# Score groups in pairs, one FFN sum bank and one projection per pair of steps in a macaron block on one core

## What is computed

```
x = x + 0.5 * ffn(layernorm(x), w_gate_up, w_proj)       # FFN "A"
x = x + attention(layernorm(x), Wq, Wk, Wv, Wo)          # sliding window of 128, blocks of 128 tokens
x = x + 0.5 * ffn(layernorm(x), w_gate_up, w_proj)       # FFN "C", the same weights

ffn:       gate, up = split(x @ w_q(gate_up).T);  h = silu(gate) * up
           out = rms_norm(h) @ w_q(proj).T
attention: scores of a block of 128 queries against the keys of its own and the block before
           (the first block of each 512 tokens only against its own), mask, softmax, times v, @ Wo.T
```

## Time and profile before

| | |
|---|---|
| median of 3 runs | 2030.6 us (2028.21 to 2031.13) |
| profiled execution | 2030.56 us, span 2028.7 us |
| PE busy | 1919.7 us, 95% |
| PE weight loads | 898.9 us, 44% |
| DVE busy | 1541.2 us, 76% |
| ACT busy | 1493.1 us, 74% |
| POOL busy | 510.9 us, 25% |
| mean granted TensorE clock | 0.980 of 2.4 GHz |

### The profile page before, as it was taken

One profiled execution on the slowest core, in us unless ns is written; L12 is line 12 of the kernel. 1 busy time (PEld: TensorE's weight loads), 2 busy tenths in 40 slices (PEclk: granted clock), 3 DMA queues, 4 the chain that ended last, 5 costly groups with the idle time before them and its releaser, 6 DMA issues. The chain is left out here.

```text
span 2028.7 us, 37471 instructions
## 1 busy us (share of the span) xinstructions
PE 1919.7 (95%) x12447; PEld 898.9 (44%) x12688; DVE 1541.2 (76%) x4079; ACT 1493.1 (74%) x2871; POOL 510.9 (25%) x559
## 2 busy tenths in 40 slices
PE   6678899999999999999999999999999999999887
PEld 3353344444444444444444444444444444444332
DVE  8966788777876888777777888777786788777673
ACT  6837777777776777777776777777776777768672
POOL 2012222232223222322222223222223232221100
PEclk8889999999999999999999999999999999999898
DMA  7336888788887878777896788878886788768772
GB/s 233 121 71 112 147 153 147 132 141 159 149 156 126 156 145 153 136 145 150 154 159 125 138 155 153 149 131 154 159 155 120 141 153 165 144 120 154 131 136 52
DMA packets 1031648, 287.81 MB, mean 142 GB/s; under 512 B 1016096, under 2 KB 1017120, under 8 KB 1030944
## 3 DMA queue, kind: packets, MB, share of 16 engines
q1 hardware_dynamic: 1031456, 285.41, 75.9%
HBM read 25.17 MB, written 8.39 MB: 17 GB/s over the span
## 5 line engine op out<-in xcount | busy, mean ns | idle before, releaser
L731 ACT ACTIVATE masked<-masked,exp_bias,exp_scale 128x256 f32<-128x256 f32 (+1 forms) x1024 | 503.8, 562 | 8.6
L1095 PE MATMUL ps_yy<-wp_t,ht 128*128 128x512 bf16 x1978 | 481.0, 383 | 14.4 <-DMA ht<-hh 11.7
L1049 PE MATMUL ps_gu<-wgu_t,xt_A 128*128 128x512 bf16 x1940 | 473.8, 382 | 11.2 <-DVE hid L859 2.5
L1049 PE MATMUL ps_gu<-wgu_t,xt_C 128*128 128x512 bf16 x1958 | 472.6, 379 | 5.3 <-DMA xt_C<-xh 0.5
L605 ACT ACTIVATE hh<-hid 128x512 f16<-128x512 f32 x256 | 161.0, 629 | 276.3 <-DVE hid L865 271.0
L876 DVE CUSTOM_DVE_ANT_0 masked<-ps_s,mask 128x256 f32<-128x256 f32 (+1 forms) x1024 | 337.4, 385 | 0.7 <-PE ps_s L1085 0.6
L865 DVE SCALAR_TENSOR_TENSOR hid<-ps_gu,h_scale_u,hid 128x512 f32<-128x512 f32 x252 | 188.9, 750 | 185.0 <-PE ps_gu L1049 184.7
L1095 PEld LDWEIGHTS ps_yy<-wp_t,ht 128*128 128x128 f16 x2016 | 197.9, 99 | 254.5 <-DMA ht<-hh 13.5
L1049 PEld LDWEIGHTS ps_gu<-wgu_t,xt_A 128*128 128x128 f16 x2048 | 198.6, 98 | 243.3 <-issue 6.3
L1049 PEld LDWEIGHTS ps_gu<-wgu_t,xt_C 128*128 128x128 f16 x2048 | 193.4, 98 | 222.5 <-issue 2.4
L850 DVE TENSOR_TENSOR prob<-masked,prob 128x1024 f16<-128x1024 f32 (+1 forms) x256 | 278.9, 1089 | 2.4 <-ACT prob L743 2.4
(11 more groups left out here) (148 smaller groups left out, 1892.8 us busy)
## 6 DMA issues: line engine op xcount, KB each, us to landing
stream<-in_L_attn_x_dram SPq DMA_DIRECT2D x32, 256.0 KB, 3.3
pt<-prob SPq DMA_TRANSPOSE x512, 3.2
out_dram<-stream SPq DMA_DIRECT2D x32, 256.0 KB, 2.4
prob<-in_L_ffn_w_gate_up_dram SPq DMA_DIRECT2D x4, 1024.0 KB, 5.6
ht<-hh SPq DMA_TRANSPOSE x256, 3.3
stream<-in_L_ffn_w_gate_up_dram SPq DMA_DIRECT2D x3, 1024.0 KB, 5.6
stream<-in_L_ffn_w_proj_dram SPq DMA_DIRECT2D x2, 1024.0 KB, 4.9
prob<-in_L_ffn_w_proj_dram SPq DMA_DIRECT2D x2, 1024.0 KB, 4.8
```

Of the source, the lines that this page charges most:

```text
L731: t = act.activation(p, p, ACT.Exp, bias=exp_bias[:, 4 * g + h:4 * g + h + 1], scale=exp_scale[:, 0:1])
L1049: t = pe.matmul(bank[:, :], xt[s][:, part, k, :], wgu_t[:, k, at:at + CH], start=(k == 0 and part == 0), stop=(k == KD - 1 and part == 1))
L1095: t = pe.matmul(ps_y[s][:, :], ht[:, n % HRING, i, :], wp_t[:, 4 * c + i % 4, :], start=(c == 0 and i == 0), stop=(c == NC - 1 and i == 2 ...
```

## The change

It issues the scores of two groups, g even and g + 1, together at the end of every odd step, the first into the two banks of ps_s, the second into ps_x and ps_m. ps_x is the bank that C's sum had; both FFNs now sum in ps_y, and the first down of a block waits for the addition of the block before. ps_m is also the projections' bank: the projections move to even steps (Q 8, K 10, V 12, output 22), wait for the maxima of both groups, and scores wait until the projection of the step before has been taken. Values stand in mid-step, between down and up. DVE's order in a step becomes: low half of the projection or its addition, maxima of the even group, low half of the output, gate's product, low half of the probabilities, maxima of the odd group, normalising, FFN addition, product with up, LayerNorm statistics, low half of hidden. Normalising stands in the step of the values. The output's split, transpose and projection stand in one step (22), and SP issues its transpose ahead of the probabilities'. Cut to its core:

```diff
-    Q_AT, K_AT, V_AT = 8, 9, 11
+    Q_AT, K_AT, V_AT = 8, 10, 12
     SCORES = 12
     PROB = SCORES + 1
     PV = SCORES + 2
-    NORM = PV + 1
-    SPLIT_O, WO_AT = NORM + 7, 23
-    LN_C, XHAT_C, SPLIT_C = 24, 25, 26
+    NORM = PV
+    SPLIT_O, WO_AT = NORM + 8, 22
+    LN_C, XHAT_C, SPLIT_C = 23, 24, 26
-    LAST_WO = 8 * LAST + WO_AT
+    LAST_WO = 8 * LAST + WO_AT + 1
...
-        ps_y = {"A": ps_yy[:, 0:CH], "C": ps_yy[:, CH:2 * CH]}
+        ps_y, ps_x = ps_yy[:, 0:CH], ps_yy[:, CH:2 * CH]
         ps_om = psum("ps_om", [P, 2 * CH])
         ps_o, ps_m = ps_om[:, 0:CH], ps_om[:, CH:2 * CH]
+        ps_sc = ((ps_s[:, 0:CH], ps_s[:, CH:2 * CH]), (ps_x, ps_m))
...
+                b = block_at(step, SPLIT_O)
+                if b is not None:
+                    sp.wait_ge(d_ol, b + 1)
+                    need(sp, p_wo, b)
+                    transpose(ot[:, :, :, :].rearrange("p a b c -> p (a b) c"), flat(oh[:, :, :]), t_o)
                 b, g = group_at(step, PROB)
...
-                if block_at(step, SPLIT_O) == LAST:
-                    output_hi(LAST)
+                b = block_at(step, SPLIT_O)
+                if b is not None:
+                    output_hi(b)
                 s, b, c, n = gate_at(step)
                 if s:
                     tanh_half(s, b, c, n)
...
+                b = block_at(step, WO_AT + 1)
+                if b is not None and b < LAST:
+                    add_output(b)
+
+                b, g = group_at(step, SCORES)
+                if b is not None and g % 2 == 0:
+                    masked_max(b, g)
+                b = block_at(step, SPLIT_O)
+                if b is not None:
+                    take_lo(oh[:, 1, :], o_norm[:, :], oh[:, 0, :], a_oh, b + 1, d_ol)
...
+                s, bf, c, n = gate_at(step)
+                if s:
+                    gated(s, bf, c, n)
+
+                b, g = group_at(step, PROB)
+                if b is not None:
+                    need(dve, t_pl[g % 2], 16 * (4 * b + g // 2))
+                    take_lo(prob_part(prob[:, g % 2, 1, :, :, :], b), prob_f32(b, g),
+                            prob_part(prob[:, g % 2, 0, :, :, :], b), a_ph, 8 * b + g + 1, d_pl)
+                b, g = group_at(step, SCORES)
+                if b is not None and g % 2 == 0:
+                    masked_max(b, g + 1)
+                b, g = group_at(step, NORM)
+                if b is not None and g % 2:
+                    normalise_o(b, g // 2)
...
+                b = complete("A", step, 2)
+                if b is not None:
+                    add_ffn("A", b, d_x1)
+                b = complete("C", step, 2)
+                if b is not None:
+                    add_ffn("C", b, d_x3)
...
-            def output_projection(b):
+            def output_projection(b, step):
                 pe.wait_ge(t_o, 16 * (b + 1))
                 need(pe, d_v, min(b + 2, NB))
                 need(pe, d_x2, b)
-                project(O, ot, p_wo)
+                need(pe, d_mx, 2 * groups_by(step + 1, SCORES))
+                project(O, ot, p_wo, ps_m)
+
+            def projections_taken(step):
+
+                for offset, done in ((Q_AT, d_q), (K_AT, d_k), (V_AT, d_v), (WO_AT, d_x2)):
+                    b = block_at(step, offset)
+                    if b is not None:
+                        pe.wait_ge(done, b + 1)
...
-                        need(pe, d_x1 if s == "A" else d_x3, b)
+                        _, s0, b0, _ = QUARTERS[place(step - 2) - 1]
+                        pe.wait_ge(d_x1 if s0 == "A" else d_x3, b0 + 1)
                     down(s, b, c, place(step - 2))
...
-                s, b, c = ffn_at(step)
-                if s:
-                    if sb_:
-                        pe.wait_ge(d_h[sb_], 4 * bb + cb + 1 + (NC if sb_ == "A" else 0))
-                    up(s, c, 1, ps_u)
-
-
-                b, g = group_at(step + 1, SCORES)
-                if b is not None:
-                    if step + 1 == SCORES:
-                        pe.wait_ge(a_lo, 8)
-                    need(pe, d_mx, 2 * groups_by(step, SCORES))
-                    if g == 0:
-                        pe.wait_ge(t_q, 16 * (b + 1))
-                        pe.wait_ge(t_k, 16 * (b + 1))
-                    scores(b, g)
 
                 b, g = group_at(step, PV)
...
+                s, b, c = ffn_at(step)
+                if s:
+                    if sb_:
+                        pe.wait_ge(d_h[sb_], 4 * bb + cb + 1 + (NC if sb_ == "A" else 0))
+                    up(s, c, 1, ps_u)
+
+
+                b, g = group_at(step + 1, SCORES)
+                if b is not None and g % 2 == 0:
+                    if step + 1 == SCORES:
+                        pe.wait_ge(a_lo, 8)
+                    need(pe, d_mx, 2 * groups_by(step, SCORES))
+                    projections_taken(step - 1)
+                    if g == 0:
+                        pe.wait_ge(t_q, 16 * (b + 1))
+                        pe.wait_ge(t_k, 16 * (b + 1))
+                    scores(b, g, ps_sc[0])
+                    scores(b, g + 1, ps_sc[1])
...
                 b = block_at(step, K_AT)
                 if b is not None:
                     pe.wait_ge(a_q, b + 1)
                     pe.wait_ge(d_q, b + 1)
-                    project(K, xt["B"], p_k)
+                    need(pe, d_mx, 2 * groups_by(step + 1, SCORES))
+                    project(K, xt["B"], p_k, ps_m)
...
```

More of the change, by code:

```diff
@@ L298, in macaron @@
         assert len(AT_STEP) == len(GATES) == 2 * NB * NC - NC
+        assert all(QUARTERS[n][1:3] == QUARTERS[n - n % NC][1:3] for n in range(len(QUARTERS)))
         def gate_at(step):
@@ L946, in step_of, with add_output @@
             def step_of(step):
[L947 to L953, removed]
+                def add_output(b):
+                    dve.wait_ge(p_wo, b + 1)
+                    dve.scalar_tensor_tensor(out=slot(b), in0=ps_m[:, :], scalar=out_scale[:, 0:1], in1=slot(b),
+                                             op0=ALU.mult, op1=ALU.add).then_inc(d_x2, 1)
                 b = block_at(step, Q_AT + 1)
@@ L993, in step_of @@
                         attention_weight(n)
-                b = block_at(step, WO_AT + 1)
-                if b is not None and b < LAST:
-                    add_output(b)
+                b = complete("A", step, 2)
[4 more added lines that the diff above has]
+                    add_ffn("C", b, d_x3)
                 s, bf, c = ffn_at(step)
@@ L1012, in step_of @@
                                       ALU.subtract, ALU.mult).then_inc(d_xh, 1)
-                b = block_at(step, SPLIT_O)
-                if b is not None and b < LAST:
-                    output_lo(b)
-                b = complete("A", step, 2)
-                if b is not None:
-                    add_ffn("A", b, d_x1)
-                b = complete("C", step, 2)
-                if b is not None:
-                    add_ffn("C", b, d_x3)
                 b = block_at(step, LN_B)
@@ L1069, in attention_weight, with project, scores @@
                 t.then_inc(a_tr, 1)
-            def project(m, tokens, done):
+            def project(m, tokens, done, bank):
                 for k in range(KD):
                     for n, (part, w) in enumerate(((0, wat_hi), (0, wat_lo), (1, wat_hi))):
-                        t = pe.matmul(ps_m[:, :], tokens[:, part, k, :], w[m][:, k, :], start=(k == 0 and n == 0),
+                        t = pe.matmul(bank[:, :], tokens[:, part, k, :], w[m][:, k, :], start=(k == 0 and n == 0),
                                       stop=(k == KD - 1 and n == 2))
                 t.then_inc(done, 1)
-            def scores(b, g):
+            def scores(b, g, banks):
                 at_block = b % BPS
@@ L1250, in step_of @@
                     pe.wait_ge(a_k, b + 1)
+                    pe.wait_ge(d_q, b + 1)
                     pe.wait_ge(d_k, b + 1)
+                    need(pe, d_mx, 2 * groups_by(step + 1, SCORES))
                     if b == 0:
                         pe.wait_ge(a_lo, 8)
-                    project(V, xt["B"], p_v)
+                    project(V, xt["B"], p_v, ps_m)
                 b = block_at(step, WO_AT)
                 if b is not None and b < LAST:
-                    output_projection(b)
+                    output_projection(b, step)
             for step in range(FIRST_STEP, STEPS):
```

37 lines of the change are left out of this document (10 added, 27 removed).

## The result

The changed kernel takes 2213.4 us in the median of four runs (2212.3 to 2215.3), the kernel before 2030.8: a ratio of 1.0912, 95% interval 1.0898 to 1.0926. It is slower, as forecast, but by 183 us and not by 116; 2213 lies above the range of 2065 to 2200. The profiled execution took 2213.36 us with a span of 2211.3 us and a mean granted clock of 0.973.

The account below looks back on a forecast made before the run. The matrix engine's own list of work was taken as the bound. Waits of 131 us in 28 blocks plus 12 at the ends, less 27 saved at score bursts, added 116 to 2030.56: 2147 us, range 2065 to 2200.

Parts of the forecast that it names:

- Q: Projection in step 0 of 8: LayerNorm statistics lengthen the vector engine's chain to 12.71, a wait of 0.89 us.
- K: Projection in step 2 of 8: the C norm's copy delays the tanh and gate's product, a wait of 1.40 us.
- the first scores' wait for k: Scores of a block's first pair, odd step 3: k's transpose lands after they are due, a wait of 0.72 us.
- the output's 1.86: Output projection, step 6 of 8: its transpose, made in the same step, is seen at 13.68 against 11.82, 1.86 us.
- the first: Rival: the clock falls at the output projection once a block, 43 us more, 2190 us; chance 0.18.
- The third rival: Nothing saved at the score bursts, waits as forecast: 2174 us; chance 0.08.
- the second: Rival: only the transfers make the matrix engine wait, the maxima being in time: 2072 us; chance 0.12.
- the fourth: Rival: the waits vanish altogether and the 27 us saving is kept, 2004 us; chance 0.05.
- 0.05 to be seen: Time allowed from the end of the maxima or a transpose until the waiting matrix engine sees it: 0.05 us.
- lands 4.3 us later in the median: k's transpose before a block's first scores: 4.3 us from issue to landing, with bounds 4.2 and 5.9.
- There Q, K and V don't wait and the output 0.56 less: 2.0: Every fourth block, with half-width score groups: shorter maxima and probabilities cut the block's waits from 5.55 to 2.0 us.
- For the 16 pairs at both ends I estimate the plain 0.7 each, 12: Step pairs in the kernel's emptier first and last steps: 0.7 us of waiting each, 12 us, possibly 0 to 30.

Follow-up runs that it names:

- e2: Changed kernel with k transposed in two DMAs, the first two groups' heads first with their own semaphore: 2202.0 us.
- e8: Changed kernel with four reorderings and their new waits mended (2073.2 us), then even-group scores issued apart in three pairs of four: 2101.8 us.
- e7: Kernel before the change with only the shared bank for both FFN sums: 2027.9 us, ratio 0.9996.
- e10: Changed kernel with four reorderings and their new waits mended, plus the output split and transposed a step earlier: 2044.5 us, ratio 1.0077.
- e3: Changed kernel with the output projection issued behind the next step's gate matmuls: 2167.8 us.
- e1: Changed kernel with the gate's product behind both groups' maxima in even steps: 2187.0 us.
- e4: Changed kernel with the even group's maxima taken at the end of the odd step, ahead of hidden's low half: 2275.8 us.

## Why the prediction failed, step by step

**Right.** The cause, a projection that shares a bank with the second group's scores; its chain on the vector engine (free at 8.18: 8.16; the tanh late in K's step: 9.96 for the 10.06 given); the first scores' wait for k and V's overlap with it (e2); the output's 1.86 (1.80 in the block shown, 1.90 in the mean); 0.21 a pair of bursts (0.20 in e8); one bank at nothing (e7); the order of a step, 6.23. The engines kept their idle shares, so it was order and not load, and e10 shows that another order takes nearly all of it away. Of the rivals the first happened at one output projection of the 28 and not at each:

```profile
1480.34 4.45 PE L1073 MATMUL ps_om<-wo,ot 128*128 128x512 f16 x12 [2.07 <-DMA ot<-oh]
```

The 42 other idle times of 1.36 to 1.98 us ahead of a projection between 280 and 1950 us were followed by full speed. The third rival is refuted by e8, the second by the table of waits, and the fourth by the time.

**Wrong.** The terms of the sum: all the waits but V's came out too small, the ends most of all, and two things were put at nothing that were not. Mean waits, forecast and measured over the middle (start to start, 27 intervals, of which 7 have half the score columns):

| | forecast, ordinary block | measured, ordinary | forecast, mean | measured, mean |
|---|---|---|---|---|
| Q | 0.89 | 1.18 | 0.67 | 0.87 |
| K | 1.40 | 1.47, mostly 1.61 | 1.05 | 1.22 |
| first scores | 0.72 | 1.27 (0.79 to 2.68) | 0.72 | 1.35 |
| V | 0.68 | 0.40 (0 to 0.81) | 0.51 | 0.33 |
| output | 1.86 | 1.85 | 1.72 | 1.90 |

1. *"0.05 to be seen"*, and the chain laid end to end: 0.15 from the last maxima to the projection, 0.11 between the low probabilities and the maxima, and the maxima end 1.47 and not 1.37 after they begin (1055.52 to 1056.99). Together 0.3 at a projection that waits for the vector engine; Q and K show 0.2 to 0.3.
2. *"lands 4.3 us later in the median"*: in the middle of the kernel after the k transpose lands in 4.7 in the median (4.3 to 5.7); it was mostly issued 2.07 after the projection, as forecast. The upper bound of 5.9 stood in the text; the value taken was that of a queue whose neighbours the change moves: a store and a load now stand right ahead, and the issue itself takes 2.9 us in the median where it took 1.9. That they cause it isn't shown. In some blocks it was more, and twice the clock fell behind it, here and at 643.40:

```profile
1524.59 0.40 PE L1083 MATMUL ps_s<-kt,qt 48*128 48x256 f16 x4 [2.63 <-DMA kt<-k]
...
1525.29 3.38 PE L1048 MATMUL ps_gu<-wgu_t,xt_C 128*128 128x512 bf16 x8
```

3. *"There Q, K and V don't wait and the output 0.56 less: 2.0"*: in every fourth block they wait 4.3 in sum: the output 2.0 (forecast 1.30), the first scores 1.6 (0.72), K 0.5 and V 0.1 (none). A quarter of 2.3 is 0.6 a block, 15 us, part of which is points 1 and 2 again. An output projection of such a block:

```profile
909.67 0.29 PE L1083 MATMUL ps_s<-kt,qt 48*128 48x128 f16 x4
...
910.00 1.90 PE L1048 MATMUL ps_gu<-wgu_t,xt_C 128*128 128x512 bf16 x8
...
917.49 2.76 PE L1073 MATMUL ps_om<-wo,ot 128*128 128x512 f16 x12 [1.93 <-DMA ot<-oh]
```

```profile
913.04 1.08 DVE L850 TENSOR_TENSOR oh<-o_norm,oh 128x512 f16<-128x512 f32 x1
```

The forecast made the vector engine's work shorter there and not the matrix engine's: the burst lasts 0.33 and not 0.54 us, so all behind it is due 0.21 sooner. And the output's low half takes 1.08 us and not 0.69 in each of these blocks; why isn't shown. K's wait stays because its gate's product still waits for the late tanh (0.60 us at 943.21), which the forecast had for the ordinary K alone.
4. *"For the 16 pairs at both ends I estimate the plain 0.7 each, 12"*: the ends cost 43 us where the forecast has 13, the largest error of one term. The last three intervals, first the kernel after, then the one before (columns as in the earlier trace rows):

```profile
1986.17:2164.93 178.76, 140.07 (x941) 63.54 (x941) 111.54 (x296) 110.55 (x208) 22.95 (x29) 0.89 0.64 119
```

```profile
1831.78:1980.25 148.47, 127.22 (x888) 57.54 (x899) 108.52 (x293) 106.88 (x200) 21.70 (x28) 0.93 0.76 139
```

The matrix engine idles 39 us there instead of 21, and at a lower granted clock. Over both ends it waits 29 us for row maxima (13.7 up to 285 us, 15.6 from 1987 on), but the kernel before waits 14.8 in the same stages, at its scores: so the maxima cost 15 more, near the 12 forecast. Waits for transposes and of the values make about 20 more, and the clock up to 14; neither was in the term. Its bounds (0 to 30) came from no row, though the shorter steps at the ends were to be seen in the kernel before.
5. The clock, which the sum had at its old level: the mean of 0.973 over 2211 us against 0.980 over 2029 is 60 us lost against 41, so 19 us more, at most, since a low clock costs nothing while the engine idles. 5 of them lie in the middle (three stretches, behind idle times of 2.07, 2.20 and 2.63 us), the rest at the ends.

So the 67 us missed come out: in the middle, where 37 are missing, 27 are the waits (5.67 a block for 4.66, times 27), 4 the values' waits (0.16 a block, put at nothing) and 5 the clock; at the ends 30, of which up to 14 are the clock. Neither part alone would have left the range of 2065 to 2200. The mechanism was right and the size was not: the step that failed is the sum of the waits, its ends first. "The waits don't undo each other" held for e3, but the product moved in e1 gave K's projection time that the first scores partly took back, so the terms of the sum are not what each edit would give back.

## What to carry to other kernels

Before two results share a bank, write down which engine must read the first and what is queued ahead of that read: here a burst saving of 27 us was bought with a wait of the matrix engine, the one engine without slack, on an engine that had a quarter of its time idle but nothing idle at that moment. A chain laid end to end over several engines needs the step from each to the next (0.1 to 0.15 us here), the queue's neighbours as they will be, and a count of its own for the first and last blocks, where less work covers it. And one part of a change alone can cost more than within it (53 us for the values' place alone, 3 us inside), so parts measured singly don't add up.

## What was not expected of the hardware

- **The clock after an idle time.** In the middle of the kernel after, 42 idle times of 1.36 to 1.98 us ahead of a projection left the granted clock at full level and one of 2.07 did not; ahead of scores 2.20 and 2.63 us lowered it, and 2.69 did not. In e1 one of 1.95 us ahead of a projection lowered it and one of 1.96 did not, and in e4 14 of 26 of 2.34 to 4.02 us ahead of the output projection did. In these runs the length of a single idle time did not settle it between 1.9 and 2.7 us. A fall made a projection up to 1.7 us longer, 4.3 instead of 2.6. The Trainium skill (TensorE: Matmul & The Clock Gate, Part 1: The HAM clock gate) has the array throttled by default and released by activity; these rows agree.
- **DMA issue in a queue.** One queue issues transposes one after another, 1.23 us for a hidden one and 2.9 for k's (medians of the kernel after). In e4, where hidden's stands ahead of the output's, the output's is issued 0.83 us after its data are ready and the projection waits 0.8 us longer; the queue's order wasn't changed alone.
- **Gains that come back.** In e1 1.9 us a block less of waiting for maxima gave back only 0.5 a block; the rest came back at the first scores (0.65), the values (0.38) and in the clock (up to 0.44).
